# Two images through a shifted convolution and a Hadamard product: another division of the setup, later loads, and ScalarE's DMA queue for the rows of x1

## What is computed

```python
gn(v):  normalise each group of 12 channels of an image (32 groups), eps 1e-5
displace(v, offset):              # 48 slots of 8 channels each
    off_px = offset * 64; off_int = round(off_px); sub = off_px - off_int
    shift each slot's channels by off_int (zeros outside), then
    convolve each channel with its slot's 3x3 Gaussian, centred at sub
hadamard(v): over channels: pad 384 to 512, times H512 / sqrt(512), keep 384
x = x + displace(gn(x), offset)   # called x1 below
x = x + hadamard(gn(x))
```

## Time and profile before

| | |
|---|---|
| Median of 3 runs | 270.97 us (267.46 to 272.32) |
| The profiled execution | 266.63 us, of it span 264.6 us |
| Busy: TensorE matmul, VectorE, ScalarE, GpSimd | 178.2, 166.8, 127.3, 68.7 us |
| Mean granted TensorE clock | 0.893 of full speed |
| HBM read and written | 60.89 MB and 29.88 MB |
| Transfers of x1 to scratch, issue to landing (median): units 0 and 1, unit 2 | 6.9, 5.7 us |

### The profile page before, as it was taken

The page is one execution under the profiler, slowest core; times in us unless marked ns, Lnnn a source line. Parts: engine busy times, 40 slices in busy tenths (PEclk is TensorE's granted clock), DMA queues, the critical chain, the costliest instruction groups (busy, mean ns, idle before and its releaser), DMA issues.

```text
span 264.6 us, 3915 instructions
## 1 busy us (share of the span) xinstructions
PE 178.2 (67%) x1228; PEld 93.7 (35%) x1228; DVE 166.8 (63%) x417; ACT 127.3 (48%) x183; POOL 68.7 (26%) x89
## 2 busy tenths in 40 slices
PE   1300038600799999568399996828799978899962
PEld 1300026500335655323147553303355644333321
DVE  2779858968465787826557885235797865455330
ACT  0198057950317793659539728459371021422111
POOL 0179000233840013078000021670000037700000
PEclk9999999965599999759769998695999995999998
DMA  6999999994648597944899969594898957545453
GB/s 198 394 416 408 301 248 378 407 394 110 175 109 282 152 362 259 367 140 151 206 363 301 411 227 366 190 377 158 252 289 334 370 214 236 180 161 206 191 235 161
DMA packets 23625, 70.64 MB, mean 267 GB/s; under 512 B 5952, under 2 KB 6976, under 8 KB 23024
## 3 DMA queue, kind: packets, MB, share of 16 engines
q1 hardware_dynamic: 18480, 60.90, 66.1%
q0 software_dynamic: 5120, 9.45, 10.8%
HBM read 60.89 MB, written 29.88 MB: 343 GB/s over the span
## 4 chain that ended last, share of the span: by engine, by line
PE 46%; DVE 21%; DMA 14%; issue 8%; ACT 8%; POOL 2%; DVEq 0%; POOLq 0%; SPq 0%; ACTq 0%
PE ps L841 18%; PE ps L823 8%; DMA x_rows<-plain 7%; PE ps L830 7%; PE ps L744 6%; DMA ring<-x_rows,index 5%; DVE halves L1064 5%; DVE ring L1298 5%; PE ps L725 4%; ACT junk L571 3%; ACT junk L574 2%; POOL x_rows L491 2%; ACT parts L631 1%; DVE plain L1155 1%; PE ps L753 1%
## 5 line engine op out<-in xcount | busy, mean ns | idle before, releaser
L1298 DVE SCALAR_TENSOR_TENSOR ring<-ps,out_bias,ring 128x1024 f32<-128x1024 f32 x32 | 41.0, 1282 | 27.7 <-PE ps L841 18.3
L622 ACT ACTIVATE ring<-ps,out_bias 128x1024 f32<-128x1024 f32 x16 | 17.8, 1113 | 68.7 <-PE ps L841 68.7
L830 PE MATMUL ps<-parts,had_sb 128*128 128x512 f16 x128 | 33.6, 399 | 16.7 <-DVE ring L1298 8.4
L841 PE MATMUL ps<-ring,w_fold 128*128 128x512 f32 x64 | 38.6, 733 | 6.1 <-DVE ring L1298 6.1
L823 PE MATMUL ps<-ring,w_a 128*128 128x512 f32 x64 | 33.8, 654 | 6.0 <-issue 3.3
L571 ACT ACTIVATE junk<-ring 128x1024 f32<-128x1024 f32 x30 | 34.3, 1142 | 4.0 <-DMA ring<-x_pad 2.7
L574 ACT ACTIVATE junk<-ring 128x1024 f32<-128x1024 f32 x30 | 34.5, 1149 | 1.0
L488 POOL DMA_DIRECT2D x_rows<-plain x8 | 4.9, 616 | 106.5 <-DVE plain L1155 106.5
L841 PE MATMUL ps<-ring,w_c 128*128 128x512 f32 x64 | 32.4, 630 | 0.0
L498 POOL DMA_INDIRECT ring<-x_rows,index x24 | 24.4, 1018 | 30.2 <-issue 30.2
L631 ACT ACTIVATE parts<-ring,scale 128x1024 f16<-128x1024 f32 x16 | 17.9, 1141 | 28.7 <-PE ps L830 14.9
(11 more groups left out here) (153 smaller groups left out, 192.6 us busy)
## 6 DMA issues: line engine op xcount, KB each, us to landing
ring<-x_pad SPq DMA_DIRECT2D x16, 1536.0 KB, 12.1
out<-ring SPq DMA_DIRECT2D x48, 512.0 KB, 5.2
shifted<-x_pad SPq DMA_DIRECT2D x32, 128.0 KB, 6.9
plain<-x_pad SPq DMA_DIRECT2D x32, 128.0 KB, 6.5
x_rows<-plain POOLq DMA_DIRECT2D x8, 512.0 KB, 6.9
shifted<-x_pad SPq DMA_DIRECT2D x16, 32.0 KB, 2.0
plain<-x_pad SPq DMA_DIRECT2D x16, 32.0 KB, 4.6
x_rows<-plain POOLq DMA_DIRECT2D x16, 32.0 KB, 5.7
```

Source lines behind the costliest of these rows:

```text
L830: last = pe.matmul(ps[n % 2][:, h, :], had_sb[:, 128 * sign:128 * (sign + 1)], parts[:, n % 2, part, s, 512 * h:512 * (h + 1)], start=Fals ...
L841: last = pe.matmul(ps[n % 2][:, h, :], weight, ring[:, 2, place_of(n), 512 * h:512 * (h + 1)], start=False, stop=True, skip_group_check=True)
L1298: dve.scalar_tensor_tensor(ring[:, t, place_of(n), :], pixels_of(ps[n % 2]), out_bias[:, q % 2, t, b:b + 1], ring[:, t, place_of(n), :], A ...
```

## The change

Five things change together. (1) ScalarE issues the transfers of `leave`, between its own instructions, instead of GpSimd. (2) In the setup GpSimd computes group ids, two tap products and the masks; VectorE's ids by column come after `unit_scales(0)`; its first statistics come earlier, its aggregates all in `means`; ScalarE runs a one-element Exp at the start and takes tile 1 of image 0 ahead of the real one. (3) Unit 1 of quarter 0 (g = 1) uses PSUM pairs of its own, `ps[0]` and `ps[1]`. (4) `dve_tiles` gives VectorE 21 tiles instead of 18, among them tiles 0 and 1 of the third image of quarters 2 and 3; the fourth image's statistics go behind result(n, 1). (5) SP's `rows_back` waits only for k = 0, and where j = 2 the load comes after it. The branch for more than nine slots keeps its work.

```diff
 def dve_tiles(i):
-    if i < 2 * QUARTER:
-        return (0, 1) if i < QUARTER + 2 else (0,)
-    return (0, 1) if i % QUARTER == QUARTER - 1 else ()
+    q, b = i // QUARTER, i % QUARTER
+    return (((0,), (0, 1), (0, 1), (0, 1)), ((0, 1), (0, 1), (0,), (0,)))[q][b] if q < 2 else ((), (), (0, 1), (0, 1))[b]
...
+        def turned_of(g):
...
+            return ps[0] if g == 1 else turned
+
+        def summed_of(g):
+            return ps[1] if g == 1 else summed
...
-                    for k in range(2):
-                        sp.wait_ge(gathered[t][k], 16 * (q + 1))
+                    sp.wait_ge(gathered[t][0], 16 * (q + 1))
...
-                if n >= 1 and n - 1 + RING < BATCH:
+                if n >= 1 and n - 1 + RING < BATCH and j != 2:
                     load(n - 1 + RING)
...
                     rows_back(w + 1)
+                    load(n - 1 + RING)
                     fetch(w + 2, 1)
...
-            pool.wait_ge(sums_in_done, 16)
-            pool.tensor_copy(sum_w[:, :, :], sums_in.rearrange("p (n c) -> p n c", c=128)).then_inc(sums_ready, 1)
-            pool.wait_ge(ids_ready, 1)
...
+            pool.wait_ge(geo_in, 16)
+            pool.wait_ge(sel_ready, 1)
+            link(pool.tensor_scalar(group8[:, :, :], bc(sel[:, 0:FAST, 0:1], [128, FAST, BIND]), float(BIND), None, ALU.mult))
+            link(pool.tensor_tensor(group8[:, :, :], group8[:, :, :],
+                                    bc(geo_of("c8").rearrange("p (o c) -> p o c", o=1), [128, FAST, BIND]), ALU.add))
+            link(pool.tensor_scalar(group8[:, :, :], group8[:, :, :], 1.0 / GROUP, -5.5 / GROUP, ALU.mult, ALU.add))
+            link(pool.tensor_scalar(group8[:, :, :], group8[:, :, :], ROUND, None, ALU.add))
+            link(pool.tensor_scalar(group8[:, :, :], group8[:, :, :], ROUND, None, ALU.subtract))
             for t in range(CT):
...
             last.then_inc(to_unit_ready, 1)
+            pool.wait_ge(sums_in_done, 16)
+            pool.tensor_copy(sum_w[:, :, :], sums_in.rearrange("p (n c) -> p n c", c=128)).then_inc(sums_ready, 1)
             pool.wait_ge(taps_ready, 1)
+            pool.tensor_tensor(taps[:, 0:FAST, 0:32], taps[:, 0:FAST, 0:32], bc(norm[:, 0:FAST, 0:1], [128, FAST, 32]), ALU.mult)
+            link(pool.tensor_tensor(taps[:, 0:FAST, 35:41], taps[:, 0:FAST, 35:41], bc(norm[:, 0:FAST, 1:2], [128, FAST, 6]), ALU.mult))
...
+            pool.tensor_tensor(view[:, 0:FAST, 0:CHUNKS], bc(geo_of("row").rearrange("p (o d) -> p o d", o=1), [128, FAST, CHUNKS]),
+                               bc(sel[:, 0:FAST, 2:3], [128, FAST, CHUNKS]), ALU.subtract)
...
+                               bc(view[:, 0:FAST, CHUNKS:], [128, FAST, CHUNKS]), ALU.mult).then_inc(view_ready, 1)
             pool.wait_ge(had_in, 16)
+            pool.wait_ge(columns_ready, 1)
...
-            for u in range(UNITS):
-                leave(u)
             gather(0)
             for n in range(1, QUARTER):
                 weights(n)
             for n in range(BATCH - QUARTER):
                 w, j = n // QUARTER, n % QUARTER
                 if j == 1:
-                    for u in range(UNITS):
...
+            def leave(g):
+                q, u = unit_of(g)
+                act.wait_ge(x1_ready, g + 1)
+                if SLOTS_OF[u] > 1:
+                    act.dma_start(x1_unit(q, u), plain[:, u, :]).then_inc(x1_out[u], 16)
+                else:
+                    for r in range(BANDS):
+                        act.dma_start(x1_unit(q, u).rearrange("p (r n) -> p r n", r=BANDS)[:, r, :],
+                                       plain[32 * r:32 * r + 32, u, 0:WIDTH_OF[u]]).then_inc(x1_out[u], 16)
...
             act.wait_ge(cleared, 1)
+            act.activation(act_scrap[:, :], accum[:, 0, 0, 0, 0:1], ACT.Exp)
+            for t in act_tiles(0):
+                take_stats(0, t)
             act.wait_ge(exp_in, 1)
             act.activation(taps[:, 0:FAST, :], taps[:, 0:FAST, :], ACT.Exp, scale=-2.0).then_inc(exp_done, 1)
-            for i in range(QUARTER):
+            for i in range(1, QUARTER):
                 for t in act_tiles(i):
                     take_stats(i, t)
             root_first(0)
             for u in range(UNITS):
                 centre(u)
             active = act.value_load(count_i[0:1, 0:1], min_val=0, max_val=OFFSETS)
+            take_stats(4, 2)
+            take_stats(5, 2)
+            leave(0)
+            take_stats(6, 1)
+            leave(1)
+            leave(2)
             more_blocks(0)
-            for i in range(QUARTER, 2 * QUARTER):
-                for t in act_tiles(i):
-                    take_stats(i, t)
+            take_stats(6, 2)
             root_second(0)
             weights(0)
             weights_c(0)
+            take_stats(7, 1)
+            take_stats(7, 2)
             high(0, 0)
...
                 result_c(n + 1)
+                if units:
+                    leave(g)
                 if stats_next:
                     take_stats(ahead, 2)
                     take_stats(ahead + 1, 0)
+                if units:
+                    leave(g + 1)
+                    leave(g + 2)
                 result_c(n + 2)
                 if stats_next:
...
-                    take_stats(ahead + 2, 0)
+                    take_stats(ahead + 2, 2)
                 if units:
                     high(n + QUARTER, 0)
                     high(n + QUARTER + 1, 0)
                 if stats_next:
-                    take_stats(ahead + 2, 1)
-                    take_stats(ahead + 2, 2)
                     take_stats(ahead + 3, 2)
...
-                if g:
-                    pe.wait_ge(masked, g)
+                if g > 1:
+                    pe.wait_ge(masked, 1 if g == 2 else g)
...
-                    if g:
+                    if g > 1:
                         pe.wait_ge(x1_ready, g)
...
+            def all_slots():
+                dve.wait_ge(ranked, 1)
+                dve.tensor_copy(sel_all[:, :, :], summed[:, 0, 0:5 * OFFSETS].rearrange("p (v k) -> p v k", v=5))
+                link(dve.tensor_copy(rank_f[:, :], summed[:, 1, 0:CT]))
+                stats_at[0] = take_stats(0)
+
+            def group_columns():
                 link(dve.tensor_tensor(pick_s[:, :, :], sel_all[:, 0:1, 0:UNITS * PER_UNIT].rearrange("p o (u s) -> p (o u) s", u=UNITS),
                                        geo_of("s4").rearrange("p (u s) -> p u s", u=UNITS), ALU.mult))
                 link(dve.tensor_reduce(group_col[:, :], pick_s[:, :, :], AX.X, ALU.add))
                 link(dve.scalar_tensor_tensor(group_col[:, :], group_col[:, :], float(BIND), geo_of("c_of"), ALU.mult, ALU.add))
                 to_group_ids(group_col[:, :], link)
-                nothing().then_inc(ids_ready, 1)
+                nothing().then_inc(columns_ready, 1)
...
+            for i in range(1, QUARTER):
+                stats_at[i] = take_stats(i)
             means(0)
             spread_means(0)
             unit_moments(0)
             unit_scales(0)
+            group_columns()
             index_rows()
+            mask(0)
             keep_moments(0)
-            mask(0)
-            take_stats(4, (0,))
             mask(1)
-            stats_at[4] = take_stats(4, (1,))
-            take_stats(5, (0,))
+            stats_at[4] = take_stats(4)
+            active = dve.value_load(count_i[0:1, 0:1], min_val=0, max_val=OFFSETS)
             add(0)
             mask(2)
-            stats_at[5] = take_stats(5, (1,))
             add(1)
             add(2)
             all_moments(0)
             second_shift(0)
             second_scale(0)
             fold_weights(0)
-            stats_at[6] = take_stats(6)
-            stats_at[7] = take_stats(7)
+            for i in range(QUARTER + 1, 2 * QUARTER):
+                stats_at[i] = take_stats(i)
...
                 result(n, 1)
                 if units and w:
+                    stats_at[QUARTER * q + 3] = take_stats(QUARTER * q + 3)
                     means(q)
...
+                result(n + 3, 1)
                 if units:
                     second_shift(q)
-                result(n + 3, 1)
...
-                    stats_at[ahead + 3] = take_stats(ahead + 3)
+                    stats_at[ahead + 2] = take_stats(ahead + 2)
```

More of the change, by code:

```diff
@@ L483, in _ @@
         def _(pool):
-            def leave(g):
-                q, u = unit_of(g)
-                pool.wait_ge(x1_ready, g + 1)
-                if SLOTS_OF[u] > 1:
-                    pool.dma_start(x1_unit(q, u), plain[:, u, :]).then_inc(x1_out[u], 16)
-                else:
-                    for r in range(BANDS):
-                        pool.dma_start(x1_unit(q, u).rearrange("p (r n) -> p r n", r=BANDS)[:, r, :],
-                                       plain[32 * r:32 * r + 32, u, 0:WIDTH_OF[u]]).then_inc(x1_out[u], 16)
             def gather_rows(q, slots):
@@ L1084, in means @@
                                               square[:, here, :], ALU.mult, ALU.subtract))
```

(4 more changed lines are left out.)

98 lines of the change are left out of this document (49 added, 49 removed).

## The result

The changed kernel took 266.76 us at the median of 20 runs (262.71 to 269.96), the kernel before 268.91 beside it (266.09 to 274.54): 2.2 us less, where 9.9 us had been forecast. The ratio is 0.9887, 95% interval [0.9844, 0.993]: a gain of about 1%. Medians here are of all runs; ratios compare only the runs in the faster of the two states that both kernels show, so the two need not agree exactly. Run again later, 12 times, it took 267.33 against 267.44: 0.9971 [0.9934, 1.0009], which does not exclude that nothing was gained. The forecast's 261.1 us stood on the three runs of the kernel before, 270.97; from the 268.91 of twenty runs the same sum would have given 259.0.

What follows compares the result with a forecast made beforehand. The prediction took the hand-overs between quarters, rather than any engine's work, to bound the kernel. Gains of 3.6+1.6+3.6+1.1=9.9 us from the 270.97 us median gave 261.1 us, range 254 to 269.

Steps and rivals of the forecast that it cites:

- Setup and convolution: Quarter 0 up to its last add: work leaves VectorE's setup, unit 1's transposes get own PSUM; last add at 50.7, 2.9 earlier.
- Start: First hand-over: rows land in 4 us, gather at 57.5, `low` at 66.9 directly behind VectorE's own work; 3.6 us gained.
- Quarter 1 to 2: Second hand-over: load 11 waits for the gather's first half, rows land after 3.2, result at 128.7 instead of 130.28; 1.6 us.
- Quarter 2 to 3: Third hand-over: load 15 leaves the gather's way, lands at 180.6, result at 184.8 instead of 188.37; 3.6 us gained.
- Quarter 3: Last quarter: result(11,1) moves ahead of `second_shift`, so result(11,0) comes near 219.7 instead of 220.84; 1.1 us gained.
- The clock: Rival, behind hand-overs: shorter waits let two or three product stretches run at 2.4 GHz; 3.6 to 5.4 more, 256.5 us; chance 0.14.
- The second rival: Hand-overs: ScalarE's queue brings nothing, landings stay 6.2 to 6.9, postponed loads cost; gain 3.4, 267.6 us; chance 0.20.
- the signs named: Wrong if bands take over 6 us, ScalarE's issues over 1, masks come after 38, or load 11 or 15 takes over 9.
- the third rival: ScalarE stalls on its own queue, 3.6 us for each of three leaves a quarter; slower, 286.8 us; chance 0.06.

Runs made afterwards that it cites:

- the copies: Follow-up kernels, mostly the changed kernel with one or more further edits, a few the kernel before with one edit; medians from 261.91 to 268.69 us.
- SP as before: Changed kernel, but loads 11 and 15 issued before the stores again and both gather halves waited for; x1 rows on ScalarE's queue: 265.38 us, 0.9841.
- the setup alone: Changed kernel keeping only setup, second PSUM home and division of statistics; x1 rows on GpSimd's queue, SP's loads and waits as in the kernel before: 265.74 us, 0.9854.
- the last copy: Changed kernel with x1 rows on GpSimd's queue, loads 8 and 9 after the first gather, load 15 landed before the fetch behind it: 261.91 us, 0.9685.

## Why the prediction was wrong, step by step

- **Setup and convolution, last add 2.9 us earlier.** Right in mechanism, and more: 4.4. `add(0)` began at 43.18 for 44.7 (the terms that the prediction gives for it, 43.8 and 0.5, make 44.3). The shifted rows of unit 0 landed at 33.9, not 34.9, masks were ready at 24.0 (25 to 26 forecast), the register load showed 0.2 idle and not 0.5.
- **Start, 3.6 us. Failed.** The step was "Landing takes 1.7 to 6.9; I take 4 [...] Gather at 57.5 (1.2 after), tile 1 landed near 65". Rows took 6.5, but being issued 1.7 us sooner than I had thought (50.6 for 52.3) they delayed the gather by only 0.9, to 58.4. The rest is the gather's own landing: its transfers took 6.2 to 8.9, tile 1 came at 68.5 for 65, and `low` at 69.8 for 66.9. I had taken that landing, 3.1 to 5.0, as a constant, although that row's longest is 11.0 and although it was measured at 63.5 us, behind loads 8 and 9, and was to be moved 5 us forward into them. The bound beside it was wrong too: with rows at 6.9, "tile 1 lands near 67 and at most 0.5 is lost", but 2.9 us more make 67.9 of 65, and `low` follows `high` by 1.2, which is over 2 lost. The other half of the step, `low` at 66.9 by VectorE's own work, is confirmed at 65.0 to 66.4 by the copies.
- **Quarter 1 to 2, 1.6 us.** Half right: 0.9. Rows in 3.0 us (3.2 forecast), and load 11 issued even 1.4 us sooner after result(0,0) than forecast; but it took 10.2 us instead of 8.4. The fetch issued behind it is the likely reason: 8.4 with that fetch held, in one trace, 8.2 to 10.5 without, 9.3 on average, in fourteen.
- **Quarter 2 to 3, 3.6 us. Failed**: 1.0 lost, 4.6 off. The step was "load 15 issued 172.2, landed 180.6". Rows took 5.8 instead of 4.4, behind issues of 1.2 to 1.4 us, and load 15 was issued 1.2 us later after result(4,0) than forecast; it took 11.5 us instead of 8.4, which is 3.1; and 4.5 instead of 4.2 from there to the result. The 8.4 was load 11's in the kernel before (load 15's own was 8.8), with no such fetch right behind it: again a price taken from a place that the change left. Of the 3.1 the copies give 1.5 to the fetch; the rest is within the scatter of such landings.
- **Quarter 3, 1.1 us.** Right in mechanism: from result(9,1) to result(11,0) it takes 25.5 us instead of 27.0. The 2.0 lost just before, at the lower clock, hide it.
- **The clock.** The rival had it add 3.6 to 5.4 us of gain. It went the other way: 1.8 us lost behind the third hand-over, where TensorE waits 4.4 us for `means` (6.7 in the later execution) instead of 0.67; in the copies with SP as before and with the setup alone it waits 2.3 and the products take 3.61 and 3.78. A hand-over that still waits, only elsewhere, still lets the clock fall. The 1.4 at the end are chance.
- **The second rival, 267.6 us**, was nearest, and by the signs named: rows over 6 us in the first hand-over, loads over 9. The two signs of the third rival came in small: issues up to 1.86 us, VectorE waiting for ScalarE; moving that wait away gave no time back. I had given the second rival 0.20. It was right that the queue brings nothing and wrong that the rows land as slowly everywhere: they land fast where a load has left and slowly where it hasn't, in 1.9 to 3.3 us against 5.5 to 6.5 on ScalarE's queue and in 2.0 to 2.6 against 5.4 to 6.3 on GpSimd's. The Trainium skill, DMA: Bandwidth & Descriptors, section "Issuing engines are not separate DMA queues", says that the transfers of all issuing engines run on the same 16 DMA engines and interleave; these rows agree.
- **What stays open.** The copies explain the start and part of quarter 2 to 3. That all cures together bring the 9.9 us of the forecast is not shown: the last copy took 261.91 us, 8.1 less than the 270.02 of the kernel before beside it, in six runs.

## What to carry to other kernels

In this kernel a DMA's time to landing went with its place in the traffic (the same gather 3.1 to 4.4, 6.2 to 8.9 and 3.8 to 5.2 us), not with the transfer alone: before a step is moved, ask what is in flight at its new place, and price it there. A start that comes earlier needs the loads ahead of it made lighter as well; here the same two loads cost 1.5 us before the change, which the next hand-over took back when they were moved, and 3 to 4 us of trace after it. And a postponed load has a new deadline: here result(8,0) started 4.49 us after load 15 had landed, and every delay of that landing, the fetch behind it included, went into it.

## What the hardware showed that I had not expected

- The same kind of issue (an x1 row of 32 KB) costs a steady 0.50 to 0.54 us on GpSimd, while on ScalarE's queue it varies from 0.34 to 1.86 us in one kernel.
- The 108 short matmuls with unused results raised the granted clock of an execution from 0.865 to 0.904 into 0.909 to 0.929 (six runs); the median was 2 to 3 us lower, which the intervals do not settle.
- Four fp32 products at the end of the kernel took 1.98 us in one execution and 3.48 in another of the same copy, both behind a wait of 1.38 us.
- Load 15 with the same fetch behind it landed after 8.4 us in one execution of a kernel and after 9.8 in another; over all such traces after 7.7 to 11.5. One trace's landing is a draw, not a price.
